# One graph layer on one core: the second bias is added to x in four large pieces near the start, not in 25 small ones along the way

## The reference, cut to what matters

```python
# x: 6250 x 64 f32, src/dst: 206250 int32 (dst is sorted), edge_attr: 206250 x 64 f32
h   = maximum(layernorm(x), 0)                     # no scale, no shift
msg = h[src] + edge_attr
agg = segment_sum(msg, dst, num_segments=6250)
out = x + relu(agg @ W1 + b1) @ W2 + b2            # W1 64 x 128, W2 128 x 64
```

## Time and profile before

| What | Value |
|---|---|
| Median of 3 runs | 531.18 us (528.41 to 531.21) |
| The profiled execution | 530.76 us |
| Its span in the profile | 529.1 us (1.66 us lie around it) |
| Mean granted TensorE clock | 0.997 |
| PE matmul busy | 470.9 us (89%) |
| DVE busy | 432.1 us (82%) |
| ACT busy | 352.9 us (67%) |
| POOL busy | 283.3 us (54%) |
| POOL L507 (`add_bias`) | 44.1 us in 25 instructions, mean 1769 ns |
| Chain that ended last | PE 87%, DVE 5%, DMA 3%, issue 2%, ACT 2% |

### The profile page before, as it was taken

The page is one execution under the profiler, slowest core; times in us unless marked ns, Lnnn a source line. Parts: engine busy times, 40 slices in busy tenths (PEclk is TensorE's granted clock), DMA queues, the critical chain, the costliest instruction groups (busy, mean ns, idle before and its releaser), DMA issues.

```text
span 529.1 us, 27474 instructions
## 1 busy us (share of the span) xinstructions
PE 470.9 (89%) x12541; PEld 417.4 (79%) x12541; DVE 432.1 (82%) x481; ACT 352.9 (67%) x503; POOL 283.3 (54%) x223
## 2 busy tenths in 40 slices
PE   1013799899999999999999999999999999998996
PEld 1002698789888989888888988988898898887885
DVE  4989997888888888888789788889889889858650
ACT  3837676676776677767767767767777777775720
POOL 4489993565275465547547547555754754216000
PEclk9999999999999999999999999999999999998999
DMA  9657139636455364553644635546464454633300
GB/s 203 178 151 226 46 112 233 192 109 191 114 146 162 110 177 127 141 166 106 172 139 118 189 111 148 155 125 183 107 179 131 140 168 111 188 97 106 93 7 9
DMA packets 139623, 73.62 MB, mean 139 GB/s; under 512 B 23644, under 2 KB 137550, under 8 KB 139382
## 3 DMA queue, kind: packets, MB, share of 16 engines
q1 hardware_dynamic: 136105, 65.30, 44.8%
q0 software_dynamic: 3168, 4.90, 2.9%
q10 hardware_dynamic: 234, 1.65, 1.0%
HBM read 66.98 MB, written 4.86 MB: 136 GB/s over the span
## 4 chain that ended last, share of the span: by engine, by line
PE 87%; DVE 5%; DMA 3%; issue 2%; ACT 2%; POOL 0%; SPq 0%; ACTq 0%; DVEq 0%
PE sum_ps L821 27%; PE sum_ps L843 19%; PE count_ps L808 19%; PE sum_ps L829 14%; PE head_ps L858 3%; PE head_ps L865 3%; DVE lo_hot L654 2%; DMA comb_rows<-counts 1%; PE turn_ps L793 1%; DVE hi_hot L654 1%; DMA dst_sb<-in_dst 1%; ACT counts L324 1%; DMA ell<-comb_rows,ell_idx 1%; ACT counts L326 1%; DVE h_parts L620 1%
## 5 line engine op out<-in xcount | busy, mean ns | idle before, releaser
L386 ACT CAST counts<-count_ps 128x784 bf16<-128x784 f32 x391 | 298.6, 817 | 98.3 <-PE count_ps L808 98.3
L654 DVE TENSOR_TENSOR lo_hot<-iota_lo,codes 128x4096 bf16<-128x4096 bf16 x98 | 224.4, 2290 | 43.5 <-ACT codes L353 31.7
L821 PE MATMUL sum_ps<-counts,h_parts 128*128 128x256 bf16 (+1 forms) x1225 | 151.2, 273 | 3.5 <-issue 3.5
L488 POOL DMA_INDIRECT ell<-comb_rows,ell_idx x50 | 76.8, 1536 | 135.5 <-DVE ell_idx L626 101.2
L808 PE MATMUL count_ps<-hi_hot,lo_hot 64*128 64x49 bf16 x6256 | 123.7, 183 | 17.4 <-DVE hi_hot L654 12.9
L808 PEld LDWEIGHTS count_ps<-hi_hot,lo_hot 64*128 64x128 bf16 x6256 | 100.6, 94 | 40.0 <-DVE hi_hot L654 13.8
L821 PEld LDWEIGHTS sum_ps<-counts,h_parts 128*128 128x128 bf16 x1225 | 112.2, 98 | 23.6 <-issue 5.1
L468 POOL DMA_INDIRECT g<-in_dst,row_i x49 | 99.5, 2031 | 55.4 <-DVE e_hot L668 39.9
L843 PE MATMUL sum_ps<-e_hot,edges 128*64 128x24 f32 x3528 | 118.2, 214 | 0.0
L843 PEld LDWEIGHTS sum_ps<-e_hot,edges 128*64 128x64 f32 x3528 | 118.2, 138 | 0.0
L654 DVE TENSOR_TENSOR hi_hot<-iota_hi,codes 128x1600 bf16<-128x1600 bf16 x98 | 101.1, 1032 | 0.0
(11 more groups left out here) (107 smaller groups left out, 221.9 us busy)
## 6 DMA issues: line engine op xcount, KB each, us to landing
edges<-in_edge_attr SPq DMA_DIRECT2D x98, 576.0 KB, 5.6
h_rows<-h_sb SPq DMA_DIRECT2D x1, 1568.0 KB, 9.7
x_sb<-in_x SPq DMA_DIRECT2D x4, 384.0 KB, 10.2
out<-o_sb SPq DMA_DIRECT2D x24, 64.0 KB, 3.7
comb_rows<-counts ACTq DMA_DIRECT2D x1, 1443.8 KB
dst_rows<-in_dst SPq DMA_DIRECT2D x49, 18.0 KB
ell<-comb_rows,ell_idx POOLq DMA_INDIRECT x50, 4.7
g<-in_dst,row_i POOLq DMA_INDIRECT x49, 5.9
```

Source lines behind the costliest of these rows:

```text
L386: nc.scalar.copy(counts[j % 2][:, :, 0:2 * half].rearrange("p s (h i) -> p h s i", h=2)[:, :, :, 8 * u:8 * u + 8], count_ps[g % 2][:, :, 0 ...
L488: nc.gpsimd.indirect_dma_start(out=ell[j % 2][0:rows, h, :, :].rearrange("p s w -> p (s w)"), out_offset=None, in_=comb_dram[:, :], in_off ...
L654: return nc.vector.tensor_tensor(out_ap.rearrange("p i (a t) -> p i a t", t=2), bc(table_ap.rearrange("p (o a t) -> p o a t", o=1, t=2), [ ...
L821: nc.tensor.matmul(sum_ps[m % 2][:, 0:cols], parts[:, s, 0:2 * F], counts[m % 2][:, s, 0:cols], start=(s == 0), stop=False, skip_group_che ...
```

## The change

`b2_all` gets a semaphore and a DMA of its own, issued by SP right behind the loads of x and ahead of the loop over double tiles. `load_weights` issues four DMAs, not five. `add_bias` now takes a slice number and adds b2 to all tiles of that slice. The adds for slices 0, 1 and 2 (128 x 768 elements each) stand on POOL between `place_ranges(0)` and the wait for `comb_out`; the one for slice 3 (128 x 832) stands behind `make_rel(0)`. The 25 adds of the loop are gone, and `add_rows` waits for all four slices.

```diff
@@ block.sync
+                sp.dma_start(b2_all[:, :], b2[:].rearrange("(o f) -> o f", o=1).to_broadcast([P, F])).then_inc(b2_in, 16)
+
                 def load_edges(t, first):
@@ load_weights
                     sp.dma_start(b1_col[:, :], b1[:].rearrange("(p o) -> p o", o=1)).then_inc(w_in, 16)
-                    sp.dma_start(b2_all[:, :], b2[:].rearrange("(o f) -> o f", o=1).to_broadcast([P, F])).then_inc(w_in, 16)
@@ block.gpsimd
-                def add_bias(f):
-                    tiles = slice(2 * f, 2 * f + tiles_in(f))
-                    pool.wait_ge(mean_sub, SLICES)
-                    pool.wait_ge(w_in, 80)
-                    nc.gpsimd.tensor_tensor(x_sb[:, tiles, :], x_sb[:, tiles, :],
-                                            bc(b2_all[:, :].rearrange("p (o f) -> p o f", o=1), [P, tiles_in(f), F]),
+                def add_bias(s):
+                    at = slice(CUTS[s], CUTS[s + 1])
+                    pool.wait_ge(mean_sub, s + 1)
+                    pool.wait_ge(b2_in, 16)
+                    nc.gpsimd.tensor_tensor(x_sb[:, at, :], x_sb[:, at, :],
+                                            bc(b2_all[:, :].rearrange("p (o f) -> p o f", o=1), [P, CUTS[s + 1] - CUTS[s], F]),
                                             ALU.add).then_inc(bias_added, 1)
@@ the loop on gpsimd
                     if j == 0:
                         place_ranges(j)
+                        for s in range(SLICES - 1):
+                            add_bias(s)
                         pool.wait_ge(comb_out, 48)
                     gather_slots(j)
                     if 1 <= j < LAST:
                         place_ranges(j)
                     if j >= 1:
                         make_rel(j - 1)
-                    if j >= 2:
-                        add_bias(j - 2)
-                add_bias(DTS - 2)
-                add_bias(DTS - 1)
+                    if j == 1:
+                        add_bias(SLICES - 1)
                 make_rel(DTS - 1)
@@ add_rows, on vector
-                    dve.wait_ge(bias_added, f + 1)
+                    dve.wait_ge(bias_added, SLICES)
@@ relu on scalar, and the first hidden() on tensor
-                    act.wait_ge(w_in, 80)
+                    act.wait_ge(w_in, 64)
-                                pe.wait_ge(w_in, 80)
+                                pe.wait_ge(w_in, 64)
```

More of the change, by code:

```diff
@@ L196, in build_gnn_layer @@
         dst_in, next_in, w_in = sem("dst_in"), sem("next_in"), sem("w_in")
+        b2_in = sem("b2_in")
         src_in = sem("src_in")
```

## The result

The changed kernel takes 537.56 us (median of 4 runs, 537.33 to 539.74), the kernel before 530.67 us beside it (528.41 to 531.21). The ratio is 1.0145, with a 95% interval of 1.0115 to 1.0174: the change costs about 7 us. I had forecast 533.0 us and a range of 529.2 to 535.6.

A forecast was written before the change was run, and what follows sets the result against it. The prediction took a start of about 58 us waiting for tables, then PE setting the pace. Its terms, 0.6 + 1.6 + 0 = +2.2 us on the profiled 530.76 us, gave 533.0 us, range 529.2 to 535.6.

The forecast's parts named there:

- the small adds' removal: 25 adds, 44.1 us of POOL, leave the loop; claimed gain 0, since PE hardly idles in the steady stretch.
- The new DMA of b2: Issued by SP behind x; claimed to land at about 18 us, 4 us ahead of its use, cost 0.
- The three adds in the gap: In POOL's 5.19 us idle from 22.00 us: 1.5 us each, first gather of slots late, +0.6 us (0 to 1.0).
- The fourth add: Behind `make_rel(0)`, near 45 us: one DVE instruction waits for its length, +1.6 us; the other choice, a fixed 0.3.
- The rule that the prediction weighed: DVE and POOL share a port pair, locked for a whole instruction; the loser waits it out: cost, the fourth add's length.
- POOL's slide: POOL's work after the fourth add slides by up to 5.1 us, slots still land before DVE wants them: cost 0.
- Rivals 2 and 3: Rival 2: first gather of slots clearly late, 535.5 us, chance 0.18. Rival 3: b2 lands late, 535.8 us, chance 0.03.

The follow-up runs named there:

- the spread version: The changed kernel with its four large adds moved to double tiles 2, 6, 12 and 18: ratio 0.9923 on the slow chip, 1.0026 on another.
- run with halves: The changed kernel with six early adds of 384 elements instead of three of 768: ratio 1.0135 to the kernel before.

## Why the prediction was wrong

**Right.** PE sets the pace from the first sums on, and the small adds' removal gives nothing that can be told (0.9988 without any add). The new DMA of b2 was no matter: the three adds started at 22.16 us, with no wait for it. The start is where the change costs, VectorE is held up at both places that I named, and the first sums start late.

**The three adds in the gap: +0.6 forecast, +2.4 measured** at the first match. Two errors. The rate was drawn from an add of 432 elements with both operands broadcast in SBUF (2.12 ns an element at most, 1.5 us for 768); the shortest add took 1.79 us, 2.3 ns an element. The trace before held a better rate: the two adds of the very form, 0.315 us at 64 elements and 0.45 at 128, make 2.1 ns for each further element and 1.80 us at 768. The estimate from the Trainium skill (GPSIMD Engine Reference, section "Elementwise — side-by-side cycle accounting"), 1.67 us, was nearer than mine, and still short of 1.79. The larger one is a DVE instruction that I passed over: I counted one instruction with two SBUF inputs in the gap, but the `tensor_scalar` of 13 elements ahead of it waited 1.23 us as well, and the subtraction behind it another 1.55. DVE lost 2.8 us there, not 0.9, and 0.40 of it was slack. The page that I weighed says so much: the Trainium skill (SBUF — State Buffer, section "SBUF: two separate sides", and its part "Who interferes with whom") names DVE instructions in a 2-port mode beside those with two inputs, and `tensor_scalar` among those that can be in such a mode. The trace agrees: 0.17 us before, 1.40 beside the add. The first gather of slots was 1.24 us late, a little over my upper end of 1.0, and no longer what the match waited for.

**The fourth add: +1.6 forecast, +3.05 measured** at the instruction, 2.5 to 2.8 at the first sums. The add took 1.93 us instead of 1.65. That it costs its length and not a fixed 0.3 was the right choice of my two. The rest: I let one DVE instruction wait for one add, but `make_rel(0)` stands right ahead of it, and VectorE waited for both, 1.15 and 1.93 us. The rule that the prediction weighed here, the loser waits out one instruction, does not give that; nor does it fit `make_rel` alone, of which `e_hot` waited out 0.29 us with 1.1 to go. The measurements decide. Together the start lost 5.2 us against my 2.2.

**POOL's slide: cost 0 forecast, 3.9 us measured** up to the first head matmul. About 2.7 of that go with the long gather (PE's wait and the slow matmuls behind it), 1.0 do not; 2.5 came back later, which the experiments do not explain. This is the step that failed as a mechanism, not as a size. I had POOL sliding later and asked whether its slots would land in time. It was ahead instead, since VectorE was 5.2 us late: POOL stood 7.78 us for the indices, and its fresh request for the port was locked out as long as VectorE issued without a pause, 11.87 us, until VectorE itself stopped for want of what the gather was to bring. PE ran out of tables, and its clock fell. By the rule that the prediction weighed, the gather would have waited for one VectorE instruction; it waited over seven seams. Why it found no seam is open. None of my rivals had it. Rivals 2 and 3 (535.5 and 535.8 us) lay nearer to the measured 537.56 than my 533.0, but for a late first gather and a late b2, and neither happened.

**The sum again**, with what was measured: 2.4 + 3.05, less 0.25 that `match(1)` no longer waits, is 5.2; + 3.9 to the first head matmul; - 2.5 later; 6.6 us, and the span is 6.5 longer. This is a tally of one trace against one: from the first sums to the first head matmul the changed kernel took 22.8 us here and 24.2 when run again.

## What to carry to other kernels

Idle time of GpSimd is only free if VectorE's work at its side is too. In these traces the VectorE instructions that came during a large add, with two SBUF inputs or a `tensor_scalar`, lost nearly all that was left of it (the subtraction 1.55 us, with 1.7 left of the second add), and where a short GpSimd instruction stood right ahead of the add they waited out both. Put such work where another engine sets the pace (the spread version cost at most 0.5%), or in small pieces where VectorE is on the path. And when an edit delays one engine, ask who now arrives early: an engine that has to ask anew for a shared port may wait until the other pauses, and a deliberate pause of 1 us was worth 3 to 5 here.

## What the runs showed of the hardware that I had not expected

- A gather issued by GpSimd was locked out for 11.87 us over seven seams between VectorE instructions; it ended 0.82 us after VectorE's last instruction ahead of a pause, as in all nine traces with a gather of over 6 us. It took 0.94 us where VectorE paused.
- A `tensor_scalar` on 13 f32 elements (0.17 us) waited 1.23 us for a GpSimd add.
- A VectorE `e_hot` that asked with 1.1 us of GpSimd's `make_rel` left lost 0.29 us when a small add stood behind (kernel before, 61.74 us), but 2.76 when a large one did (spread, 61.20 us).
- Adds of 768 and 832 f32 elements on GpSimd take 1.79 to 1.93 us when not held up, 2.3 ns an element, and those of 384 elements 0.98 us (run with halves): an estimate from 384 and 768 is 2.1 ns for each element and 0.17 us besides.
- A pause of PE of 1.17 us, which ended at 75.73 us, was followed by 3 us (from 76.50) at a mean granted clock of 0.56.
- One chip ran every version some 20 us slower, with 23 to 34 waits of some 0.4 us in the edge sums in each trace, 8 to 12 us in all, and gave ratios for small differences (0.987, 0.992) that did not hold on the other chips (0.9988, 1.0026).
